# The features' product as seven block products, laid between the second half's gated blocks

## The reference

```
xn = layernorm(x)                                        # over the 256 columns
# attention part: rfs = random features
dot(v)   = v @ (xis[:, None] * proj).T                   # 256 features
rfs(v)   = 1/16 * exp(xis) * exp(dot(v) - 0.5*sum(v*v) * xis*xis)
s        = rfs(xn) @ rfs(input_weights).T                # 256 x 256: "the features' product"
# gate part
h = silu(xn @ w1.T * w1_s) * (xn @ w2.T * w2_s)          # 256 -> 1024, "gated blocks"
h = gelu(h @ h1.T * h1_s)                                # 1024 -> 1024
h = gelu(h @ h2.T * h2_s)                                # 1024 -> 1024
out = x + s * silu(h @ w3.T * w3_s)                      # 1024 -> 256
```

## Time and profile before

| | |
|---|---|
| time, median of 3 runs | 1296.65 us (1296.34 to 1297.63) |
| the profiled execution's own time | 1296.85 us |
| its span, first to last instruction | 1295.0 us |
| PE busy | 1285.5 us (99% of the span) |
| DVE busy | 978.4 us (76%) |
| POOL busy | 789.4 us (61%) |
| ACT busy | 761.5 us (59%) |
| granted TensorE clock, mean | 0.998 |
| one tile on PE, gated stage to gated stage | 158.95 us (180.80 to 339.75, tile 1) |

### The profile page before, as it was taken

How to read it: one execution, slowest core, us unless ns; L and a number is a source line. 1 busy time by engine, 2 the same in 40 slices (tenths; PEclk the granted TensorE clock), 3 DMA queues, 4 the chain that set the end, 5 groups by cost and what they waited for, 6 DMA issues and landing times.

```text
span 1295.0 us, 16328 instructions
## 1 busy us (share of the span) xinstructions
PE 1285.5 (99%) x6078; PEld 1067.8 (82%) x6078; DVE 978.4 (76%) x1255; ACT 761.5 (59%) x1010; POOL 789.4 (61%) x803
## 2 busy tenths in 40 slices
PE   9999999999999999999999999999999999999997
PEld 7788888888888888888888888888888888888887
DVE  8878778778787777878778787777878777556675
ACT  4566655666556665475655656557555666565664
POOL 7974015899669994699946999379984790040000
PEclk9999999999999999999999999999999999999999
DMA  9698935555264551654417454275442744213441
GB/s 344 254 363 245 300 114 148 183 164 180 76 170 161 169 164 69 179 174 152 162 72 197 152 180 133 82 191 177 153 131 86 213 153 149 95 65 131 147 158 40
DMA packets 98197, 209.61 MB, mean 162 GB/s; under 512 B 14144, under 2 KB 17472, under 8 KB 97088
## 3 DMA queue, kind: packets, MB, share of 16 engines
q1 hardware_dynamic: 80176, 157.11, 36.5%
q0 software_dynamic: 17936, 51.39, 14.2%
HBM read 175.92 MB, written 38.83 MB: 166 GB/s over the span
## 4 chain that ended last, share of the span: by engine, by line
PE 99%; DVE 0%; ACT 0%; issue 0%; POOL 0%; POOLq 0%
PE ps L223 74%; PE ps L226 25%; DVE split L206 0%; PE ps L354 0%; PE ps L238 0%; DVE ry L206 0%; ACT split L202 0%; DVE xin L206 0%; ACT quad L202 0%; ACT xT L202 0%; POOL ident L636 0%; POOL ident L633 0%; POOL ones L634 0%; POOLq L636 0%; POOLq L1338 0%
## 5 line engine op out<-in xcount | busy, mean ns | idle before, releaser
L223 PE MATMUL ps<-split,ring 128*128 128x512 f32 x2800 | 763.6, 390 | 0.0
L223 PEld LDWEIGHTS ps<-split,ring 128*128 128x128 f32 x2800 | 525.5, 188 | 109.2 <-ACT quad L202 0.2
L206 DVE TENSOR_TENSOR split<-quad,split 128x1024 fp32r<-128x1024 f32 x258 | 340.2, 1329 | 181.0 <-ACT split L202 179.7
L226 PE MATMUL ps<-split,ring 128*128 128x512 f32 x784 | 305.0, 389 | 0.0
L202 ACT ACTIVATE split<-quad 128x1024 fp32r<-128x1024 f32 x258 | 266.2, 1051 | 42.5 <-PE ps L226 42.5
L737 POOL TENSOR_TENSOR cube<-cube,seen 128x256 f32<-128x256 f32 x176 | 223.5, 1270 | 14.1
L202 ACT ACTIVATE quad<-ps 128x512 f32<-128x512 f32 x214 | 127.0, 596 | 164.8 <-PE ps L226 164.7
L223 PE MATMUL ps<-xT,w 128*128 128x512 f32 x766 | 217.2, 391 | 0.8 <-ACT xT L202 0.8
L206 DVE TENSOR_TENSOR quad<-ps,quad 128x512 f32<-128x512 f32 x213 | 144.1, 684 | 52.1 <-ACT quad L202 33.1
L202 ACT ACTIVATE quad<-quad,cols 128x512 f32<-128x512 f32 (+1 forms) x194 | 137.5, 717 | 68.6 <-DVE quad L206 68.0
L226 PEld LDWEIGHTS ps<-split,ring 128*128 128x128 f32 x784 | 147.1, 188 | 30.5
(11 more groups left out here) (118 smaller groups left out, 1246.0 us busy)
## 6 DMA issues: line engine op xcount, KB each, us to landing
ring<-hs SPq DMA_DIRECT2D x428, 256.0 KB, 3.5
xin<-in_x SPq DMA_DIRECT2D x16, 512.0 KB, 4.3
s_h<-s SPq DMA_DIRECT2D x16, 512.0 KB, 5.9
seen<-in_h POOLq DMA_DIRECT2D x64, 128.0 KB, 2.9
ry<-in_x SPq DMA_DIRECT2D x15, 512.0 KB, 5.5
out<-ry SPq DMA_DIRECT2D x15, 512.0 KB, 2.6
z_h<-xin POOLq DMA_DIRECT2D x56, 128.0 KB, 4.4
xT<-z_h POOLq DMA_DIRECT2D x14, 512.0 KB, 6.8
```

The lines of the kernel that those rows point to most:

```text
L206: return dve.mark(lambda e: e.tensor_tensor(dst, a, b, op))
L223: pe.run(lambda e: e.matmul(dst, stat, mov, start=start, stop=stop, skip_group_check=loose))
L226: return pe.mark(lambda e: e.matmul(dst, stat, mov, start=start, stop=stop, skip_group_check=loose))
```

## The change

From the second tile on, `mix` is not called. Its work is done by `seven_mix`: seven block products of 128x128 blocks (`plain`: four float32 matmuls of 128 columns each), placed before steps 1 to 7 of the second half's gated blocks, in banks 4, 5 and 6. The features' blocks need three sums (S1, S2, S3), which DVE makes before steps 3, 4 and 5 of the first half, and one more, S4, in the second half. The weights' sums (`WT`) are made once, in the first tile. ACT copies four of the results (before steps 1, 3, 5, 6 of the second half) and DVE adds three (before 2, 5, 7). As banks 4 to 6 are taken, the second half's gated steps use banks (0, 1) and (2, 3) in turn. The first half's list is what it was. The stores of s are issued after the seventh product.

```diff
--- before.py
+++ after.py
@@ -121,6 +121,7 @@
         ab2 = sb("ab2", [P, KD])
         amp = sb("amp", [P, 3, KD])
         PS = sb("PS", [P, 4, P])
+        WT = sb("WT", [P, 4, P])
         with ExitStack() as first:
             def sf(name, shape, dt=F32):
@@ -555,8 +556,94 @@
                     mixed[h] = cast(in_rows(s[j], b // 2), ps[:, bank, :], tok, *s_free[j])
                     free[bank] = [mixed[h]]
             mix_done[h] = tok
-            sp.wait(mixed[h])
-            s_stored[j] = d_s[j].send(sp, s_h[h], s[j][:, :, :])
+            mixed[h] = [mixed[h]]
+            keep_s(h)
+        def keep_s(h):
+            sp.wait(*mixed[h])
+            s_stored[h % 2] = d_s[h % 2].send(sp, s_h[h], s[h % 2][:, :, :])
+        WB = {(k, n): WS[:, k, n * P:(n + 1) * P] for k in range(KD) for n in range(2)}
+        def sums_of_win():
+            T1, T2, T3, T4 = (WT[:, i, :] for i in range(4))
+            a = vv(T1, WB[0, 1], WB[0, 0], ALU.subtract, ws_done[0])
+            vv(T3, WB[1, 1], WB[0, 1], ALU.subtract)
+            a = vv(T2, WB[1, 1], T1, ALU.subtract, a)
+            summed["T"] = vv(T4, WB[1, 0], T2, ALU.subtract, a)
+        def seven_mix(h0, place, spare, banks):
+            h1 = h0 + 1
+            a11, a12, a21, a22 = (quad[place][:, KD * j + r, :] for j in (1, 0) for r in range(KD))
+            S1, S2 = (quad[spare][:, i, :] for i in range(2))
+            A, B, E = (ps[:, bank, :] for bank in banks)
+            c = {(i, n): s[j][:, :, n * P:(n + 1) * P] for i, j in ((1, 1), (2, 0)) for n in range(2)}
+            box = {}
+            def three(bank):
+                return bank.rearrange("p (b d) -> p b d", b=NB)
+            def plain(weights, moving, dst, first, last, *tokens):
+                pe.wait(*tokens)
+                for b in range(NB - 1):
+                    mm(dst[:, b * P:(b + 1) * P], weights[:, b * P:(b + 1) * P], moving, first and b == 0, last, True)
+                b = NB - 1
+                return mm_mark(dst[:, b * P:(b + 1) * P], weights[:, b * P:(b + 1) * P], moving, False, last, True)
+            def sum1():
+                box["S1"] = vv(S1, a21, a22, ALU.add, feat[h0], feat[h1], *quad_free[spare])
+            def sum2():
+                box["S2"] = vv(S2, S1, a11, ALU.subtract, box["S1"])
+            def sum3():
+                box["S3"] = vv(a21, a11, a21, ALU.subtract, box["S1"])
+            def p1():
+                tok = plain(a11, WB[0, 0], A, True, False, feat[h1], ws_done[0], *free[banks[0]])
+                box["c11"] = cast(c[1, 0], three(A), tok, *s_free[1])
+            def p2():
+                tok = plain(a12, WB[1, 0], B, True, True, *free[banks[1]])
+                box["c11"] = vv(c[1, 0], three(B), c[1, 0], ALU.add, tok, box["c11"])
+                free[banks[1]] = [box["c11"]]
+                box["S4"] = vv(a12, a12, S2, ALU.subtract, box["S2"])
+            def p6():
+                tok = plain(S2, WT[:, 1, :], A, False, False, box["S2"], summed["T"], box["u1"])
+                box["u2"] = cast(c[1, 1], three(A), tok)
+            def p5():
+                box["p5"] = plain(S1, WT[:, 0, :], E, True, False, *free[banks[2]])
+            def p7():
+                tok = plain(a21, WT[:, 2, :], A, False, False, box["S3"], box["u2"])
+                box["u3"] = cast(c[2, 1], three(A), tok, *s_free[0])
+                box["c22"] = vv(c[2, 1], three(E), c[2, 1], ALU.add, box["p5"], box["u3"])
+            def p4():
+                tok = plain(a22, WT[:, 3, :], A, False, True, box["u3"])
+                box["c21"] = cast(c[2, 0], three(A), tok)
+                free[banks[0]] = [box["c21"]]
+            def p3():
+                tok = plain(a12, WB[1, 1], E, False, True, box["S4"], box["c22"])
+                box["c12"] = vv(c[1, 1], three(E), c[1, 1], ALU.add, tok, box["u2"])
+                free[banks[2]] = [box["c12"]]
+                quad_free[place] = quad_free[spare] = [tok]
+                mixed[h0], mixed[h1] = [box["c21"], box["c22"]], [box["c11"], box["c12"]]
+                keep_s(h0)
+                keep_s(h1)
+            def p1_first():
+                p1()
+                box["u1"] = box["c11"]
+            return [sum1, sum2, sum3], [p1_first, p2, p6, p5, p7, p4, p3]
         s_stored = [None, None]
@@ -770,7 +857,8 @@
         act.wait(d_cols.token)
         a_ab = act.mark(lambda e: e.activation(amp[:, 0, :], xis, ACT.Exp))
-        PAIRS = [((6, 7), (4, 5), (2, 3), (0, 1))[n] for n in (0, 1, 2, 0, 1, 2, 0, 1, 3, 2, 0, 3, 1, 2, 3, 0)]
+        PAIRS = [((6, 7), (4, 5), (2, 3))[n % 3] for n in range(KH)] + [((0, 1), (2, 3))[n % 2] for n in range(KH)]
         PAIRS0 = [((6, 7), (4, 5), (2, 3))[n % 3] for n in range(2 * KH)]
@@ -1007,7 +1095,7 @@
         def gate_y(h):
             j = h % 2
-            y_tok[h] = both_of(h, yt, yt, s[j], ALU.mult, y_tok[h], mixed[h])
+            y_tok[h] = both_of(h, yt, yt, s[j], ALU.mult, y_tok[h], *mixed[h])
             s_free[j] = [y_tok[h], s_stored[j]]
         def store_y(h):
@@ -1081,6 +1169,10 @@
                         7: [lambda: silu_y(h0 - 2), lambda: gate_y(h0 - 2), lambda: store_y(h0 - 2)]}
                 for m, part in enumerate((todo[:1], todo[1:2], todo[2:3], todo[3:4], todo[4:6], todo[6:7])):
                     side[m + 2] = side.get(m + 2, []) + part
+            if t:
+                sums_f, products_f = seven_mix(h0, L0.at["v"], L0.at["t2"], (4, 5, 6))
+                for m, task in zip((3, 4, 5), sums_f):
+                    side[m] = side.get(m, []) + [task]
             L0.made["b11"], L0.made["b21"] = gated(t, h0, (L0.at["b11"], L0.at["b21"]), side)
             if t == 0:
                 sums_of_weights()
@@ -1094,6 +1186,9 @@
                     side[m] = side.get(m, []) + part
             elif t:
                 fills.append(count_odd)
+            if t:
+                for m, task in enumerate(products_f):
+                    side[m + 1] = side.get(m + 1, []) + [task]
             L0.made["b12"], L0.made["b22"] = gated(t, h1, (L0.at["b12"], L0.at["b22"]), side)
             if t == 0:
                 norms_in(1)
@@ -1120,9 +1215,10 @@
             if t:
                 for task in [split(L0, "b21", 0), split(L0, "b21", 1)] + sums[:2]:
                     task()
-            mix(h0, (4, 5), L0.at["v"])
-            mix(h1, (6, 7), L0.at["v"])
-            quad_free[L0.at["v"]] = [mix_done[h0], mix_done[h1]]
+            if t == 0:
+                mix(h0, (4, 5), L0.at["v"])
+                mix(h1, (6, 7), L0.at["v"])
+                quad_free[L0.at["v"]] = [mix_done[h0], mix_done[h1]]
             if 0 < t < NT - 1:
                 for h in (h0 + 2, h1 + 2):
                     rows_in(h)
@@ -1145,7 +1241,7 @@
                 (1, 0): [split(L1, "t2", 0)], (1, 1): [split(L1, "t2", 1)], (1, 2): [sub(L1, "t3", 0)], (1, 3): [fill, fill, fill, first_away],
                 (2, 0): [split(L1, "t1", 0)], (2, 1): [split(L1, "t1", 1)], (2, 2): [sub(L1, "t3", 1)], (2, 3): [sub(L1, "t4", 0)] + first(norms_out, h0 + 2) + first(norms_out, h1 + 2),
                 (3, 0): [split(L1, "t3", 0)], (3, 1): [split(L1, "t3", 1)], (3, 2): [sub(L1, "t4", 1)], (3, 3): [split(C, "b11", 0, 2)],
-                (4, 0): [split(L1, "b22", 0)], (4, 1): [split(L1, "b22", 1)], (4, 2): [sums_of_proj] if t == 0 else [lambda: sums_of_rows(h0 + 2)] if t + 1 < NT else [],
+                (4, 0): [split(L1, "b22", 0)], (4, 1): [split(L1, "b22", 1)], (4, 2): [sums_of_proj, sums_of_win] if t == 0 else [lambda: sums_of_rows(h0 + 2)] if t + 1 < NT else [],
                 (4, 3): [split(C, "b11", 1, 2)] + first(norms_in, h0 + 2) + first(norms_in, h1 + 2),
                 (5, 0): [split(L1, "t4", 0)], (5, 1): [split(L1, "t4", 1)], (5, 2): first(turn_blocks, h0 + 2), (5, 3): first(split_rows, h0 + 2),
                 (6, 0): [split(C, "b22", 0, C.slot)], (6, 1): [split(C, "b22", 1, C.slot)], (6, 2): first(turn_blocks, h1 + 2), (6, 3): first(split_rows, h1 + 2)}
@@ -1190,7 +1286,7 @@
             made_y[b] = cast(yt[:, b, :], yt[:, b, :], a, func=ACT.Silu)
         def gated_y(b):
-            made_y[b] = vv(yt[:, b, :], yt[:, b, :], s[0][:, b, :], ALU.mult, made_y[b], mixed[h])
+            made_y[b] = vv(yt[:, b, :], yt[:, b, :], s[0][:, b, :], ALU.mult, made_y[b], *mixed[h])
         def added(b):
             x0 = xin[0][:, b, :]
```

## The result

The changed kernel takes 1303.45 us (median of 4, 1302.35 to 1304.49) against 1297.14 for the kernel before in the same session (1296.34 to 1299.44). The ratio is 1.005, with a 95% interval of 1.0038 to 1.0062: slower by half a per cent, 6.3 us. The forecast was 1301.1, the range 1296.5 to 1306.5. The profiled execution took 1303.63 us, its span is 1301.8, 6.8 us more than before, at the same mean granted clock of 0.998.

A forecast was written before the change was run, and what follows sets the result against it. PE's steps were taken to bound the kernel. Tiles 1 to 6 add 0.81 us each (wait 1.45 less saving 0.64), tile 7 saves 0.64: +4.2 on 1296.85 gives 1301.1 us, range 1296.5 to 1306.5.

The forecast's parts named there:

- What bounds the kernel: Whole kernel: PE, busy 99% of the span, sets the time; only its own work and its waits count.
- PE's own work: Features' product: seven block products cost 6.27 us against 6.91 for the old one, saving 0.64 us per tile.
- upper end of 0.03: Switch between kinds of matmul: 0.03 us more on each block product, which would cut the saving to 0.43 us.
- weight loads aren't hidden: Rival for the block products: each short matmul takes its load's 0.190 us, giving 1324.2 us; chance 0.02.
- What DVE gets: Gated stage: S1 to S3 cost DVE 2.24 us against 0.83 of slack, so step 8's multiplication ends 1.41 us later.
- cheap sums: Rival for S1 to S3: every sum runs at 0.60 us, PE waits only about 1.0, total 1298.4 us; chance 0.24.
- Who waits for it: Step 10's second bank: PE waits 1.45 us for DVE's multiplication of step 8 in tiles 1 to 6.
- Later steps: Gated steps 11 and 12: multiplications of steps 9 and 10 free their banks half a microsecond early, so no second wait.
- Whose loads nobody waits for now: Stores of s move earlier on SP, past the ring's feeding; nobody waits for the ring's loads, so no cost was counted.
- After the gated stage: Third ring product: t2 ready at 390.9, needed at 391.2, so wait taken as 0, with 1.0 us as other end.
- the debt goes on: Rival at the third ring product: t2's low parts late, 1.0 us in up to 6 tiles, up to 1307.1; chance 0.14.
- The sum: Whole kernel: +0.81 us in each of tiles 1 to 6, -0.64 in tile 7, together +4.2, giving 1301.1 us.

The follow-up runs named there:

- e1: Changed kernel with S1 to S3 recorded before step 0 of the first half instead of before steps 3 to 5; 1295.06 us, ratio 0.9979.
- e2: Kernel before with three unused 128x512 sums on DVE before steps 3, 4 and 5, nothing else; 1304.11 us, ratio 1.0049.
- e3: Kernel before with the changed kernel's list of bank pairs, no sums and no block products; 1310.48 us, ratio 1.0101.
- e4: Changed kernel with the two stores of s issued in the second layer's second product; 1307.45 us, ratio 1.0076.
- e8: Changed kernel with POOL's counting held until t2 is ready, 15 pieces instead of 16, and stores of s late; 1300.54 us, ratio 1.0033.
- e10: Changed kernel with only POOL's counting held until t2 is ready, still 16 pieces per tile; 1300.34 us, ratio 1.0027.
- e5: e7 with the stores of s also moved to the sixth product of the first layer; 1293.03 us, ratio 0.9971.
- e7: e1 with POOL's counting held until t2 is ready, 15 instead of 16 pieces per tile; 1292.93 us, ratio 0.9971.
- e11: Changed kernel with 15 instead of 16 pieces counted per tile, counting not held; 1303.01 us, ratio 1.0046.
- e6: e1 with the seven block products in one stretch where the old product stood, and the old bank list; 1319.09 us, ratio 1.0176.

## Why the prediction held, point by point

- **What bounds the kernel.** Right: PE's steps are the path before, and every microsecond of the change is either PE's own work or a wait of PE.
- **PE's own work.** 128-column matmuls start (360.46 - 359.79) / 6 = 0.112 us apart, as taken from the earlier trace rows. The saving is 0.57 per tile (tile 7: 136.93 from its first gated to its first projection matmul, 137.50 before), not 0.64. A block product between gated groups costs 0.906 us (from product to product in tile 7, less 1.814 for the two groups), 0.01 more than taken and well below the upper end of 0.03. The switch between kinds can be seen, but it mostly cancels: the first three intervals after a block product take 0.78 instead of 0.68 (360.60 to 361.38), while the product's own eight take 0.81 instead of 0.896 (359.79 to 360.60). The rival "weight loads aren't hidden" is dead. A load is still recorded at 190 to 192 ns in the new group, beside 0.112 from start to start. So the sentence of TensorE: Matmul & The Clock Gate of the Trainium skill on weight loads and row groups, which the prediction kept as a rival, doesn't hold here.
- **What DVE gets.** 1.06, 0.67 and 0.67 us busy against 1.1, 0.7, 0.7 forecast: S1 meets POOL, the others don't, so the rival "cheap sums" falls in the trace itself. Step 8's multiplication is 1.45 late (forecast 1.41).
- **Who waits for it.** Place, releaser and count were right: step 10's second bank, DVE's multiplication, tiles 1 to 6, none in tile 7. The size is 1.44 in tile 2 and 1.27 to 1.31 elsewhere, forecast 1.45. The first ring step comes 1.1 us later from the tile's start than before in tile 2 and 0.9 elsewhere, of which 0.2 are the border effect; 0.8 was forecast. e1, e2 and e3 show the two parts of this step one by one: the sums make the delay, the two pairs are paid for by the two products. Later steps held, as forecast.
- **"Whose loads nobody waits for now."** This failed. Ring pieces came late to the third product in tiles 1, 2 and 5 of the profiled execution, 2.2 us together. The step rested on the trace of before, in which no load of a middle tile waits for the ring, and had no term for what the loads meet when SP's and POOL's transfers are moved against them. They are issued as early as before, but those of tile 2 took 8.6 us to land instead of 5.6; with the stores of s moved away it is 4.7 (e4).
- **"After the gated stage", taken at 0, with 1.0 kept.** The mechanism was the rival "the debt goes on", and it is partly true: 0.78 and 0.74 us in tiles 3 and 6, where the differences and a low part lay beside POOL's counting. It came in another form than forecast: t2's low parts were just in time for the third product, and it is the low parts of the next products that were late. DVE was forecast to have t2 ready 14.2 us after the first ring step (390.9 - 376.7). It took 13.0 in tile 2 (390.72 - 377.71), as both low parts ran at 1.21 and not 1.64 us, and 14.4 in tile 3. The forecast put a figure near the worst tile in the place of all, and called 0.3 us of slack a fit without looking at the products behind.
- **The sum.** e8 and e10 take away just these waits, and measure 1300.5 and 1300.3: +3.4 to 3.8 over their before (ratios 1.0027 and 1.0033), where the forecast has +4.2. The likeliest case and its mechanism were right; 2.5 to 2.9 us of the 6.3 came from the two terms at 0. The forecast was 2.1 us low. The whole still lies in the range, whose upper end was kept open for the debt; nothing in it stood for late ring pieces, so for their part that is luck.

What stays open is how the held counting makes the ring's pieces arrive in time. In tile 2 of e10 the four pieces land 7.3 us after their issue, against 8.6 in the change, with the stores of s still beside them; in e8, where the stores are late too, it is 4.3. e5 and e7, which differ in the stores alone, have 4.3 and 6.2. So the stores lengthen the pieces' way, and holding the counting takes off just enough of the rest. Holding it moves POOL's `seen` loads and its work together, and no run moved one alone. e11 only says that one piece less of counting doesn't do it.

## What to carry to other kernels

An operation that saves time on the engine that bounds must be charged on the engine that feeds it: count the slack up to the next reuse of each bank, and put the new work where that engine is idle anyway. Here the same three sums cost 1.3 us a tile in one place and nothing some 6 us earlier. And when a stage that gave cover disappears, whatever had long idle time behind it (5.5 us before) stands at the edge: hold back the work of a neighbour that could lie beside it. Test each cure alone and look in the trace for what it did, since it can do what was expected and still lose: in e4 the ring's pieces came in time, and the time got worse, as the same edit started POOL's counting earlier.

## What the runs showed of the hardware that was not expected

- In e6 a wait of 2.3 us on PE was followed, after 1.5 us of work at full clock, by about 3.4 us at the lower of TensorE's two levels (1.2 and 2.4 GHz), with 512-column matmuls 0.427 us apart instead of 0.227. The same came behind the waits of 2.07, 1.95 and 2.14 us in tiles 4, 5 and 6, but not behind the one of 2.20 us in tile 3, where the granted clock stayed at 1.00. So the length of the wait alone doesn't decide it. The gaps of up to 1.3 us in the changed kernel and 1.7 us in e3 never lowered the clock.
- Two-input DVE operations in SBUF stretch beside POOL's counting, by up to 0.54 us each (a 128x1024 difference of 1.22 us takes up to 1.76), a little more than the 0.44 of the earlier trace rows. What makes it costly is how many are hit: six 128x1024 differences took 6.89, 7.73, 8.82 and 9.69 us where the counting's first load was issued 9.2, 7.8, 5.5 and 1.7 us after the ring's first step (the change's tiles 2 and 3, e4, e6). It is POOL's work and not its load that counts: in tile 1 of e6 the load was issued 2.2 us after the ring's first step, but the work waited for it until 10.2, and the differences took 6.89. That is the contention which SBUF — State Buffer of the Trainium skill, "Who interferes with whom", states for a DVE instruction with two SBUF inputs.
- Loads of the ring take longer while the stores of s are in flight: the four 256 KB pieces of the ring took 8.6 us to land with the stores of s beside them (the change, tile 2) and 4.7 or 4.3 with the stores moved away (e4, e8). e5 and e7 differ in the stores alone, with the counting held in both: 4.3 against 6.2 us for the same pieces.
- A change of kind, from 128-column float32 matmuls to 512-column float32r ones and back, costs PE little: 0.01 us per block product in tile 7, although the first three intervals behind it are 0.1 us longer.
